# Attention over 16 images on one core: low value columns moved to an aligned offset, and a new written-out order of all tasks

## What is computed

```python
h = jnp.einsum('oc,bcn->bno', wp, xf)          # projection to q, k, v of 8 heads x 64
q = pixnorm(q) * scale; k = pixnorm(k) * scale; v = pixnorm(v)
attn = softmax(jnp.einsum('bihd,bjhd->bijh', q, k), axis=2)
res = jnp.einsum('bijh,bjhd->bihd', attn, v)
res = jnp.einsum('oc,bnc->bon', wo, res)
return (a_c * x + b_c * res) / div
```

## Time and profile before

| what | value |
|---|---|
| median of 3 runs | 3014.3 us (3014.02 to 3014.5) |
| profiled execution, its own time | 3014.43 us |
| its span, first to last instruction | 3012.6 us |
| granted clock of TensorE, mean | 0.999 |
| PE matmul busy | 2967.4 us (98%) |
| PE weight loads busy | 2021.3 us (67%) |
| DVE busy | 2586.9 us (86%) |
| ACT busy | 2368.0 us (79%) |

### The profile page before, as it was taken

One profiled execution on the slowest core, in us unless ns is written; L12 is line 12 of the kernel. 1 busy time (PEld: TensorE's weight loads), 2 busy tenths in 40 slices (PEclk: granted clock), 3 DMA queues, 4 the chain that ended last, 5 costly groups with the idle time before them and its releaser, 6 DMA issues.

```text
span 3012.6 us, 85444 instructions
## 1 busy us (share of the span) xinstructions
PE 2967.4 (98%) x36928; PEld 2021.3 (67%) x36928; DVE 2586.9 (86%) x3197; ACT 2368.0 (79%) x2993; POOL 491.1 (16%) x678
## 2 busy tenths in 40 slices
PE   6999999999999999999999999999999999999997
PEld 5766676666667666676666766667666666766664
DVE  6898898888889889898888988889888898888986
ACT  5887787877878777787777878788787787877785
POOL 0211121111211121112111121112211121111210
PEclk9999999999999999999999999999999999999999
DMA  3223324224142342433223322332322324224143
GB/s 102 52 41 69 78 51 103 54 60 93 37 103 51 65 88 40 106 58 75 65 61 85 58 75 65 72 82 51 92 60 62 87 42 102 54 61 92 33 86 92
DMA packets 459529, 211.04 MB, mean 70 GB/s; under 512 B 407952, under 2 KB 407952, under 8 KB 459152
## 3 DMA queue, kind: packets, MB, share of 16 engines
q1 hardware_dynamic: 459152, 205.58, 30.5%
HBM read 71.30 MB, written 33.55 MB: 35 GB/s over the span
## 4 chain that ended last, share of the span: by engine, by line
PE 89%; DVE 7%; issue 2%; DMA 1%; ACT 0%; POOL 0%; SPq 0%; DVEq 0%; ACTq 0%
PE ps_pv L929 23%; PE ps_score L908 21%; PE ps_dense L886 13%; PE ps_dense L890 11%; PE ps_dense L888 11%; PE ps_dense L945 4%; PE ps_dense L947 3%; PE ps_dense L946 3%; DVE probs L721 3%; DVE arena L683 1%; DVE probs L712 1%; DVE sumsq L659 0%; DMA x_res<-in_x 0%; DVE res L733 0%; PE ps_score L956 0%
## 5 line engine op out<-in xcount | busy, mean ns | idle before, releaser
L527 ACT ACTIVATE e_tile<-ps_score,shift 128x1024 f32<-128x1024 f32 x1024 | 1112.5, 1116 | 282.6 <-PE ps_score L908 273.5
L721 DVE TENSOR_TENSOR probs<-e_tile,probs 128x1024 f16<-128x1024 f32 x1024 | 1237.3, 1236 | 4.2 <-ACT probs L534 0.2
L929 PEld LDWEIGHTS ps_pv<-v_pair,probs 128*128 128x128 f16 x24576 | 782.0, 97 | 179.0 <-issue 129.6
L929 PE MATMUL ps_pv<-v_pair,probs 128*128 128x65 f16 (+1 forms) x24576 | 838.9, 193 | 10.3 <-DVE probs L721 5.7
L908 PE MATMUL ps_score<-qkT 64*128 64x512 f16 x6144 | 754.4, 378 | 8.9 <-DMA qkT<-arena 6.9
L886 PE MATMUL ps_dense<-wpT_hi,x_hi 128*128 128x512 f32 x1536 | 643.7, 419 | 2.0 <-DVE wpT_lo L792 1.8
L890 PE MATMUL ps_dense<-wpT_hi,x_lo 128*128 128x512 f32 x1536 | 603.3, 393 | 0.0
L888 PE MATMUL ps_dense<-wpT_lo,x_hi 128*128 128x512 f32 x1536 | 600.4, 391 | 0.0
L534 ACT ACTIVATE probs<-e_tile 128x1024 f16<-128x1024 f32 x512 | 543.5, 1061 | 55.1 <-PE ps_pv L929 38.9
L712 DVE CAST probs<-e_tile 128x1024 f16<-128x1024 f32 x512 | 360.3, 704 | 154.5 <-PE ps_pv L929 125.2
L908 PEld LDWEIGHTS ps_score<-qkT 64*128 64x128 f16 x6144 | 257.4, 94 | 347.1 <-issue 85.4
(11 more groups left out here) (50 smaller groups left out, 1865.5 us busy)
## 6 DMA issues: line engine op xcount, KB each, us to landing
x_raw<-in_x SPq DMA_DIRECT2D x128, 256.0 KB, 3.0
x_res<-in_x SPq DMA_DIRECT2D x128, 256.0 KB, 3.6
out<-x_res SPq DMA_DIRECT2D x128, 256.0 KB, 2.4
arena<-in_w_proj SPq DMA_DIRECT2D x24, 128.0 KB, 2.9
qkT<-arena SPq DMA_TRANSPOSE x128, 4.8
resT<-res_split SPq DMA_TRANSPOSE x128, 3.4
arena<-in_w_out SPq DMA_DIRECT2D x1, 1024.0 KB, 7.3
```

The source lines that it names most:

```text
L527: act.activation(e_tile[:, t % E_BUFS, :, :], ps_score[:, t % 2, :, :], ACT.Exp, bias=shift[:, 0:1], scale=1.0 / (QK_UP * QK_UP)).then_inc ...
L721: dve.tensor_tensor(probs_of(b, t, 1), e_tile[:, t % E_BUFS, :, :], probs_of(b, t, 0), ALU.subtract).then_inc(probs_low, 1)
L929: mm = pe.matmul(ps_pv[:, h, o:o + n], probs_of(b, t, part)[:, h, queries], v[:, cols], start=(j == 0 and it == 0 and part == 0 and cols.s ...
```

## The change

Two things change. First, `v_pair` rows become 160 float16 (320 bytes), and the low values move from columns 65 to 128 to columns 72 to 135, byte 144 of a row. Second, all tables of ticks are replaced. No task is added or taken away, and no semaphore changes. The core of the diff (tables of the other engines are replaced in the same way):

```diff
-PROJ_AT = (-1889, -1806, -1800, -1615, -1447, -1218, -1176, -1119, -1107, -722, -638, -390, -113, 30, 169, 181,
-    784, 928, 1270, 1333, 1373, 1484, 1528, 1733)
+PROJ_AT = (-1850, -1834, -1450, -1294, -1230, -1189, -1128, -1125, -955, -639, -604, -602, -41, 173, 236, 264,
+    930, 931, 934, 1421, 1714, 1715, 1716, 1860)
...
-OUT_AT = (5190, 5289, 5459, 5462, 6186, 6290, 6388, 6391)
+OUT_AT = (4979, 4982, 5600, 5738, 6157, 6340, 6601, 6647)
...
-LOAD_RES_AT = (3127, 5330, 5772, 5790, 6834, 6849, 6887, 7084)
-STORE_AT = (5708, 5771, 6819, 6832, 6855, 6873, 7094, 7450)
+LOAD_RES_AT = (3408, 4814, 5331, 5430, 5469, 5475, 6531, 7332)
+STORE_AT = (4881, 5348, 5466, 5467, 5476, 5493, 7480, 7541)
...
-FIRST_SCORE_AT = ()
+FIRST_SCORE_AT = (-3864,)
-FIRST_LOW_QK_AT = (-3640,)
+FIRST_LOW_QK_AT = (-3664,)
...
-        VCOLS = 2 * D + 1
         SUMS = D + 1
-        v_pair = sb("v_pair", [P, 4, NT, VCOLS + 1], F16)
+        LOW = D + 8
+        VCOLS = 2 * D + 32
+        v_pair = sb("v_pair", [P, 4, NT, VCOLS], F16)
...
-                dve.tensor_tensor(v[:, :, :, D + 1:VCOLS],
+                dve.tensor_tensor(v[:, :, :, LOW:LOW + D],
...
-                            for part, cols in ((0, slice(0, SUMS)), (0, slice(D + 1, VCOLS)), (1, slice(0, SUMS))):
+                            for part, cols in ((0, slice(0, SUMS)), (0, slice(LOW, LOW + D)), (1, slice(0, SUMS))):
```

More of the change, by code:

```diff
@@ L100 @@
 W_CHAINS = ((0, 4), (4, 8), (8, 16))
-SCORE_AT = (0, 31, 174, 529, 887, 1085, 1330, 1365, 1396, 1477, 1527, 1565, 1862, 2088, 2230, 2265, 2291, 2294,
-    2468, 2577, 2706, 2898, 2921, 2978, 2987, 2992, 3386, 3452, 3521, 3680, 3788, 3802)
-EXP_AT = (176, 202, 663, 671, 756, 760, 781, 789, 871, 874, 917, 928, 934, 940, 1041, 1043, 1062, 1064, 1070,
[3 rows of a table removed]
-HIGH_P_AT = (106, 501, 294, 675, 380, 786, 436, 870, 483, 875, 578, 936, 1040, 966, 1061, 1069, 1067, 1071,
[3 rows of a table removed]
-LOW_P_AT = (239, 287, 301, 314, 437, 439, 440, 465, 516, 529, 675, 776, 1041, 1054, 1074, 1103, 1129, 1316,
[3 rows of a table removed]
@@ L116 @@
-ATTEND_AT = (173, 382, 900, 945, 1339, 1345, 1422, 1520, 1539, 1619, 2087, 2089, 2246, 2289, 2293, 2460, 2492,
-    2662, 2887, 2919, 2922, 2979, 2991, 2993, 3392, 3453, 3536, 3548, 3794, 3956, 4107, 4125)
-PROJ_AT = (-1889, -1806, -1800, -1615, -1447, -1218, -1176, -1119, -1107, -722, -638, -390, -113, 30, 169, 181,
-    784, 928, 1270, 1333, 1373, 1484, 1528, 1733)
-SQUARE_AT = (-2343, -2225, -2091, -1965, -1962, -1585, -1460, -1452, -1106, -916, -302, 115, 304, 610, 676,
-    775, 872, 890, 941, 964, 1067, 1081, 1278, 1515)
@@ L122 @@
[L122 to L126, removed]
-NORM_AT = (-1087, 338, 2078)
-SCALE_AT = (-910, -766, -53, -24, 548, 572, 573, 579, 1588, 1633, 1634, 1635)
-HIGH_V_AT = (113, 120, 225, 758, 1868, 1872, 2126, 2127)
@@ L139 @@
[L139 to L143, removed]
-LOAD_RES_AT = (3127, 5330, 5772, 5790, 6834, 6849, 6887, 7084)
-STORE_AT = (5708, 5771, 6819, 6832, 6855, 6873, 7094, 7450)
+SCORE_AT = (-37, 197, 291, 387, 882, 921, 935, 1255, 1422, 1602, 1717, 1824, 1887, 2052, 2198, 2243, 2271,
+    2537, 2812, 2847, 2936, 2957, 2969, 2972, 3065, 3126, 3169, 3192, 3464, 3477, 3499, 4056)
@@ new lines @@
+EXP_AT = (-173, -2, 3, 19, 266, 636, 653, 654, 668, 670, 786, 817, 947, 949, 955, 959, 993, 996, 1039, 1077,
[3 rows of a table added]
+HIGH_P_AT = (49, 31, 55, 261, 623, 637, 668, 795, 689, 800, 730, 950, 760, 956, 778, 965, 1379, 1040, 1417,
[3 rows of a table added]
+LOW_P_AT = (51, 53, 56, 610, 643, 645, 681, 697, 704, 727, 747, 750, 771, 779, 1163, 1224, 1418, 1420, 1435,
[3 rows of a table added]
+ATTEND_AT = (332, 394, 893, 936, 1302, 1356, 1450, 1648, 1718, 1837, 1946, 2007, 2242, 2245, 2332, 2554, 2828,
+    2864, 2945, 2961, 2970, 2973, 3073, 3099, 3175, 3210, 3471, 3479, 3845, 4057, 4058, 4138)
@@ new lines @@
+PROJ_AT = (-1850, -1834, -1450, -1294, -1230, -1189, -1128, -1125, -955, -639, -604, -602, -41, 173, 236, 264,
+    930, 931, 934, 1421, 1714, 1715, 1716, 1860)
+SQUARE_AT = (-2115, -2107, -2014, -1921, -1827, -1684, -1676, -1605, -1023, -1022, -974, -227, -151, 1, 113,
+    265, 787, 951, 952, 997, 1048, 1091, 1097, 1108)
+COPY_AT = (-2108, -2095, -2013, -1829, -1826, -1680, -1242, -1054, -1011, -1005, -923, -186, 0, 2, 257, 660,
+    798, 953, 964, 1003, 1076, 1092, 1101, 1360)
+REDUCE_AT = (-2025, -1939, -1829, -1820, -1703, -1134, -1034, -853, -222, -42, -27, 24, 46, 52, 54, 57, 728,
+    751, 1182, 1421, 1423, 1465, 1474, 1495)
@@ new lines @@
+SEED_AT = (-759, 573, 1531)
+NORM_AT = (-1087, 338, 2078)
+SCALE_AT = (-109, -108, -71, -29, 683, 696, 729, 767, 1647, 1651, 1679, 1832)
+HIGH_V_AT = (-891, -234, -89, 12, 1983, 2029, 2116, 2411)
+LOW_V_AT = (21, 31, 47, 629, 2042, 2090, 2273, 3300)
+TURN_QK_AT = (-81, 717, 773, 1360, 1374, 3350, 3404, 3417)
+HIGH_QK_AT = (-1000, -263, 799, 979, 1043, 1049, 1979, 2266)
+LOW_QK_AT = (-61, 48, 715, 1164, 1419, 1449, 2277, 2433)
+TAKE_AT = (731, 1422, 1546, 2158, 2462, 3310, 3990, 4146)
+TURN_RES_AT = (1375, 3362, 3376, 3413, 3508, 4736, 4815, 5383)
@@ new lines @@
+HIGH_RES_AT = (963, 1093, 1982, 2415, 2577, 3052, 3156, 5050)
+LOW_RES_AT = (1242, 1576, 2451, 2469, 3339, 3755, 4055, 5261)
+OUT_AT = (4979, 4982, 5600, 5738, 6157, 6340, 6601, 6647)
+ADD_OUT_AT = (4740, 4756, 5299, 5512, 5717, 5749, 6199, 6252)
+FINISH_AT = (4903, 5058, 5137, 5190, 6070, 6076, 6180, 6509)
+LOAD_X_AT = (-3318, -2825, -2724, -2720, -2719, -2208, -1241, -779)
+HIGH_X_AT = (-3097, -3049, -2994, -2342, -2118, -2112, -2098, -2047)
+LOW_X_AT = (-2725, -2658, -2558, -2452, -2442, -2419, -2154, -1937)
@@ L146 @@
+LOAD_RES_AT = (3408, 4814, 5331, 5430, 5469, 5475, 6531, 7332)
+STORE_AT = (4881, 5348, 5466, 5467, 5476, 5493, 7480, 7541)
 PROJ_BANK = (1, 0, 1, 0, 1, 0, 1, 0, 1, 0, 1, 0, 1, 0, 1, 0, 1, 0, 1, 0, 1, 0, 1, 0)
 OUT_BANK = (1, 0, 1, 0, 1, 0, 1, 0)
-FIRST_SCORE_AT = ()
-FIRST_EXP_AT = ()
+FIRST_SCORE_AT = (-3864,)
+FIRST_EXP_AT = (-3536, -3528)
 FIRST_HIGH_P_AT = ()
@@ L154 @@
 FIRST_ATTEND_AT = ()
[L155 to L158, removed]
+FIRST_PROJ_AT = (-4064, -4056, -4048, -4040, -4032, -4024, -3992, -3984, -3936, -3896, -3888, -3880, -3872)
+FIRST_SQUARE_AT = (-3952, -3896, -3864, -3832, -3808, -3800, -3752, -3736, -3680, -3624, -3584, -3560, -3544)
+FIRST_COPY_AT = (-3944, -3880, -3848, -3816, -3792, -3776, -3744, -3720, -3664, -3608, -3568, -3552)
+FIRST_REDUCE_AT = (-3960, -3912, -3904, -3896, -3880, -3848, -3776, -3768, -3712, -3656, -3640)
 FIRST_SEED_AT = (-3752,)
 FIRST_NORM_AT = (-4096,)
-FIRST_SCALE_AT = (-3712, -3704, -3696, -3688)
-FIRST_HIGH_V_AT = ()
+FIRST_SCALE_AT = (-3696, -3688, -3680, -3672)
+FIRST_HIGH_V_AT = (-3616, -3600, -3592)
 FIRST_LOW_V_AT = ()
-FIRST_TURN_QK_AT = ()
-FIRST_HIGH_QK_AT = (-3608,)
-FIRST_LOW_QK_AT = (-3640,)
+FIRST_TURN_QK_AT = (-4000,)
+FIRST_HIGH_QK_AT = (-3632, -3576)
+FIRST_LOW_QK_AT = (-3664,)
 FIRST_TAKE_AT = ()
@@ L181 @@
     -3856, -3840, -3824)
-W_HIGH_AT = (-4024, -4016, -4008, -4000, -3784, -3768, -3760, -3728, -3712, -3704, -3696, -3640, -3632, -3624,
-    -3616, -3600)
+W_HIGH_AT = (-4024, -4016, -4008, -4000, -3784, -3768, -3760, -3728, -3712, -3704, -3696, -3688, -3672, -3656,
+    -3648, -3640)
 W_NORM_AT = (-4080, -3976, -3888)
-W_SCALE_AT = (-4064, -4056, -4048, -4040, -3968, -3952, -3944, -3936, -3872, -3864, -3856, -3848, -3832, -3816,
+W_SCALE_AT = (-4064, -4056, -4048, -4040, -3968, -3952, -3944, -3936, -3872, -3864, -3856, -3840, -3824, -3800,
     -3792, -3784)
[L187 to L190, removed]
+W_LOW_AT = (-4024, -4016, -4008, -4000, -3832, -3816, -3808, -3760, -3744, -3736, -3728, -3720, -3704, -3648,
+    -3632, -3624)
+W_TURN_AT = (-4096, -4088, -4080, -4072, -4016, -4008, -4000, -3976, -3968, -3960, -3952, -3944, -3928, -3920,
+    -3912, -3904)
 X_PIECES = [(ct, half) for half in range(2) for ct in range(CT)]
-FIRST_TICK = -3128
-LAST_TICK = 7450
+FIRST_TICK = -3318
+LAST_TICK = 7541
 def prepare_and_attend(nc, x, w_proj, w_out, out):
```

## The result

The changed kernel takes 2994.1 us against 3014.5 us before, a ratio of 0.9932 (95% interval 0.9918 to 0.9945): 20.4 us faster, where 42 were forecast. It is inside the forecast's range, but less than half of the forecast gain. Slow executions are left out of every time given here: those of 3252, 3672, 4134 and 5076 us show granted clocks between 0.65 and 0.85, and one of 10227 us (experiment 13) shows a clock of 1.0 and stays unexplained.

The account below looks back on a forecast made before the run. PE was taken to set the pace from 72.06 to 2909 us. From 3014.4, less 35.4 (layout) and 10.8 (order), plus 3 (waits) and 1 (ends), came 2972 us; likeliest range 2962 to 2986, 8 in 10 reaching 3000.

Parts of the forecast that it names:

- layout: Attend tasks: aligned low-value matmuls save 4.5 ns each, 72 ns a task over 492 tasks, 35.4 us off.
- joins and neighbours on PE: PE's task order: fewer costly entries into projections, joined ones free, 0.7 us a round, 10.8 us off.
- new waits in a round: Tasks behind joined projections: late exponentials hold PE 0.2 us a round, 3 us on.
- opening and end: Opening taken as 0, later final stores 1 us on; -2 to +2 for both ends.
- S11 late by 0.2 to 0.5 us: Score task after P21 and P22: ACT needs 9.3 us for its exponentials, PE arrives after 9.1, so it waits.
- Rival A: Attend matmuls: alignment isn't the cause, weight loads may set the gap; layout gives 0, 3007 us, chance 0.14.
- the rule of the 16-byte line: Low-value operand: eight 16-byte lines after, nine before, saving 3 ns each, 24 us in all, time 2983.
- My own reading: Low-value matmul: slow because its operand starts 2 bytes past a multiple of 4; aligned, it takes 29 ns.
- B: DVE and ACT take over: late probabilities or exponentials hold PE 1.5 us a round, 2992 us, chance 0.17.
- C: Runs P16 to P18 and P20 to P22 starve ACT and DVE, making the kernel slower: 3024 us, chance 0.04.
- D: Joins of projections cost as much as entries, 0.9 us a round, 2986 us; no separate chance, inside the range.

Follow-up runs that it names:

- experiment 13: Kernel before with the new layout, and three projections moved next to the one ahead of them on TensorE, other queues unchanged: 3063.4 us, ratio 1.0162.
- experiment 3: Changed kernel with one DMA issue moved: the load of image piece 5 queued on SP ahead of the store of O5: 2971.4 us, ratio 0.9855.
- experiment 1: Kernel before, old order kept, with only the new layout of the values: 3003.0 us, ratio 0.9958.
- experiment 12: Kernel before, old layout, with only the order of the opening (FIRST_ and W_ tables) taken from the change: 3005.7 us, ratio 0.997.
- experiment 2: Changed kernel with the layout's three edits undone, so the new order with the old layout: 3009.0 us, ratio 0.9979.
- experiment 6: Kernel of experiment 3 with rows of 260 bytes and the low values at byte 132: 2977.5 us, ratio 0.9876.
- experiments 4 and 5: Kernel of experiment 3 with query groups starting at multiples of 66 float32 in PSUM, no longer 65, run twice: 2968.2 and 2967.4 us.
- experiment 15: Kernel of experiment 3 with the joins of P3 and P5 undone, each put behind the next score task: 2976.2 us, ratio 0.9871.
- experiments 8 and 9: Kernel of experiment 3 with the low-value matmul cut to 32 and to 48 of 64 columns (timing probes): 2945.2 and 2944.1 us.
- experiment 11: Kernel of experiment 3 with softmax sums in one key tile of eight, 64 columns in the others (timing probe): 2963.2 us, ratio 0.9828.

## Why the prediction was wrong

The sum had four terms. Three have an experiment of their own. The joins are what experiment 3 leaves when layout and opening are taken off, so that the sum must come out at the result; the 0.7 us between them is the difference between sessions.

| term | forecast | measured | from |
|---|---|---|---|
| layout | -35.4 | -12.3 | experiment 1 |
| joins and neighbours on PE | -10.8 | -22.5 | experiment 3 less 1 and 12: 2971.4 - 3003.0 + 9.1 |
| new waits in a round | +3 | +22.8 | experiment 3 |
| opening and end | +1 | -9.1 | experiment 12 (opening alone) |
| sum | -42.2 | -21.1 | result -20.4 |

The check that doesn't hold by construction is experiment 2: for the order alone the last three terms give -8.8 us, and -6.3 were measured. The forecast promised 23 us too much from the layout and put the waits 20 us too low; it put the gain of the joins 12 us too low and that of the opening and end 10 us. That the total was only 21 us off and inside the range is partly luck, since these errors offset each other.

**Two steps failed: the one on waits, and the size of the layout term.** On the waits: I followed SP's queue at the end of the kernel, and checked bank, exponentials and probabilities for the joined projections, but priced the stores and loads within a round at nothing. That the load of piece 5 now stands behind the store of O5 could be read from the new `LOAD_X_AT` and `STORE_AT`; I left the first out even of the diff above. The term was +3 us, and experiment 3 measures 22.8. The wait didn't land at a joined projection; it landed at O6, an output projection that now follows P0 and P1 closely and needs the bank of the first. I found S11 late by 0.2 to 0.5 us instead; in the trace S11 has no wait.

**The layout helped where it was forecast to, by a third of the size.** The low matmul did fall from 33.7 to about 29 ns, as taken from the nearest row. What failed is that its neighbours would stay at 29.2: in about half of the groups the first matmul rose to 36, and 4.5 ns of gain became 1.7 a group (12.3 us for 35.4). Rival A (nothing from the alignment) is out by experiment 6, where the same matmul, with the same weights, is fast or slow by where its operand starts. The Trainium skill (SBUF — State Buffer, Specifications) has the rule of the 16-byte line, which I weighed against the rows and set aside. By the estimate of the prediction it gives 24 us (and 2984 us, not the 2983 written there); that is twice what was measured, but it named the boundary at which the low matmul changes. My own reading, a start 2 bytes past a multiple of 4, named the wrong one: at byte 132 the low matmul still takes 33 ns. The row behind both, a 65-column operand that always crosses into a ninth line and yet takes 29 ns, was the reason to set the rule aside, and I still can't explain it.

**The joins were right in kind and too small in price.** A join has no extra (0 was taken, the upper bound of 0.10 is out). But an entry costs 0.13 us after a score task and 0.10 after an attend task, since the matmuls after the first also run at 0.228 to 0.236 us and only from the seventh on at 0.2267, and I priced the run at 0.23. About 1 us a round comes from entries. The rest of the 1.5 us by which a round of experiment 3 is shorter than one of experiment 1 (183.7 to 182.2) are waits of the old order that are gone: in the trace of experiment 1, P10 is 0.2 us late after A25 and P0 0.2 to 0.3 after O5. I had not looked for them, since PE shows as busy for 184.55 of 184.60 us.

**The opening** was missed: I looked at where the first score task stands and not at `W_TURN_AT`. Of the last five weight transposes, which stood behind P12, one now goes ahead of P8 and four ahead of P9, and with them the release of the first `high_qk`. The 4.37 us transpose of the earlier trace rows is now issued at 60.54 us and runs under P11 and P12. The end was missed by little: the stores cost nothing, but from the last attend task to O7 it is 23.4 us after and 22.9 before, and the DVE-bound stretch didn't keep its length (74.5 us from A12 to A31 after, 72.6 before; 74.5 also with the order alone).

**The rivals.** B gave 2992 us for 1.5 us of waits in a round, and 1.8 were measured (O6 1.4, O7 0.35): its number was nearly right, by luck, since neither late probabilities nor late exponentials held PE, and DVE and ACT are not the bound (experiment 3 runs without them in the way). C is out: P18 and P22 have no waits, nor has what follows them. D is out by experiment 15.

**What stays open** is why about every second group has one gap of 34 to 36 ns, mostly behind its first matmul. It isn't the parity of the output's start (experiments 4 and 5), it is gone with 64 columns everywhere or with 48 in the low matmul, and it isn't in the old layout. In experiment 6 it comes back, behind the third matmul, in the two tiles where the low one is fast. A cost of weight loads alone doesn't give it. Open too are whether the low matmul's 4 to 5 ns come from its start or from the 16 bytes that it shared with the high values, and what in rows of 272 bytes slows the projections.

## What to carry to other kernels

When an order of tasks is rewritten, follow every queue that feeds a moved task, the DMA queue among them, and ask of each load what stands ahead of it that it doesn't need: one load behind one store cost 22.8 us of 2994, more than the 20.4 us that the change gained. Here the victim was the task that reused a bank a few tasks on, not the one that was joined. And price a small per-instruction gain by the group it sits in, since the group may give back only part: 4.5 ns on one of three matmuls became 1.7 on the group.

## What the runs showed of the hardware

- A float16 matmul with its own load of 128 weight columns is followed by the next after 26.6 to 27.1 ns with 32 or 48 moving columns alike (experiments 8 and 9), and after 29.2 ns with 65.
- A float16 moving operand of 128 bytes is followed after 28.3 to 28.7 ns when it starts at a multiple of 16 bytes and after 33 to 34 when it doesn't (experiment 6; in experiment 3 some aligned ones take 34 even so); with three such operands in a row, all at multiples of 16, it is 29.6 ns each (experiment 11). One of 130 bytes takes 29.2 ns at any multiple of 4 in the old layout, and 29 or 36 in the new.
- A projection of 12 matmuls in 4-byte floats takes 2.72 us behind another one, 2.82 behind an attend task and 2.85 behind a score task (experiment 3). Of the 0.13 us behind a score task, 0.11 lie behind its first matmul and the rest is spread over the next five.
